# Attention: GpSimd clamps every half tile of the attention in one instruction, VectorE only multiplies, ScalarE only exponentiates

## The reference, cut to what matters

```python
q = (embeds[rows] @ qW).reshape(e, HEADS, dh)        # 4 heads of 24
k = (embeds[cols] @ kW).reshape(e, HEADS, dh)
v = (embeds[cols] @ vW).reshape(e, HEADS, dh)
scores = jnp.clip(jnp.einsum('ehd,ehd->eh', q, k), -10.0, 10.0)
exp_s = jnp.exp(scores)
norms = segment_sum(exp_s, rows)[rows]
w = exp_s / (norms + 1e-08)
res = segment_sum(w[:, :, None] * v, rows)
```

## Time and profile before

| what | us |
|---|---|
| median of 3 runs (lowest, highest) | 1285.33 (1283.32, 1286.96) |
| the profiled execution's own time | 1289.9 |
| its span, first to last instruction | 1287.9 |
| from the attention's first clamp to the end of GpSimd's last one | 450.9 |

### The profile page before, as it was taken

The page is one execution under the profiler, slowest core; times in us unless marked ns, Lnnn a source line. Parts: engine busy times, 40 slices in busy tenths (PEclk is TensorE's granted clock), DMA queues, the critical chain, the costliest instruction groups (busy, mean ns, idle before and its releaser), DMA issues.

```text
span 1287.9 us, 23338 instructions
## 1 busy us (share of the span) xinstructions
PE 1053.3 (82%) x8352; PEld 622.0 (48%) x8352; DVE 966.7 (75%) x1603; ACT 692.6 (54%) x903; POOL 597.2 (46%) x343
## 2 busy tenths in 40 slices
PE   3878877778886788888888888994799699999893
PEld 2545545445553222222222222231569699999783
DVE  8668888896664799999999999994865654542566
ACT  7556555555533899999979898992100000001221
POOL 8442454233103799999989998995000000000000
PEclk9878888977687799999989999997899899999896
DMA  0010000000016211121111222221000100010201
GB/s 10 26 40 5 5 8 6 5 5 18 2 42 189 68 38 46 45 49 47 42 44 36 60 52 51 46 59 48 1 1 32 37 29 21 2 33 8 68 28 38
DMA packets 98907, 44.80 MB, mean 35 GB/s; under 512 B 85196, under 2 KB 96716, under 8 KB 98672
## 3 DMA queue, kind: packets, MB, share of 16 engines
q1 hardware_dynamic: 97104, 41.58, 12.2%
q0 software_dynamic: 1696, 1.74, 0.5%
HBM read 30.73 MB, written 12.56 MB: 34 GB/s over the span
## 4 chain that ended last, share of the span: by engine, by line
PE 52%; DVE 25%; issue 12%; ACT 5%; POOL 4%; another core or an unknown queue 2%; DMA 1%; SPq 0%; DVEq 0%; ACTq 0%; POOLq 0%
DVE Eb L1151 16%; PE PS L1325 16%; PE PS L553 11%; PE PS L557 8%; DVE Eb L1145 3%; PE PS L1765 3%; POOL Eb L985 3%; PE PS L1333 2%; PE PS L1075 2%; PE PS L1065 2%; ACT Eb L1116 2%; PE PS L1316 1%; ACT Eb L1118 1%; PE PS L1772 1%
## 5 line engine op out<-in xcount | busy, mean ns | idle before, releaser
L985 POOL TENSOR_SCALAR Eb<-Eb 128x1024 f32<-128x1024 f32 (+4 forms) x175 | 430.8, 2483 | 42.0 <-ACT Eb L1120 40.8
L1151 DVE SCALAR_TENSOR_TENSOR Eb<-Eb,PS 128x1024 f32<-128x1024 f32 (+4 forms) x350 | 366.8, 1084 | 16.4 <-ACT Eb L1118 10.1
L1120 ACT ACTIVATE Eb<-PS,small 128x1024 f32<-128x1024 f32 (+2 forms) x263 | 251.7, 997 | 27.2 <-PE PS L1065 23.4
L593 ACT ACTIVATE CT<-PS 128x500 f32 x313 | 183.5, 587 | 147.1 <-PE PS L557 139.3
L553 PE MATMUL PS<-mov,oneS 128*128 128x100 f16 x1565 | 187.8, 235 | 74.1 <-issue 70.5
L553 PEld LDWEIGHTS PS<-mov,oneS 128*128 128x128 f16 x1565 | 148.4, 109 | 159.1 <-issue 118.0
L1325 PE MATMUL PS<-hs,CT 128*128 128x192 f16 (+1 forms) x2500 | 213.5, 247 | 3.6 <-DVE SG L1566 1.6
L1325 PEld LDWEIGHTS PS<-hs,CT 128*128 128x128 f16 (+1 forms) x2500 | 208.1, 99 | 7.3 <-DVE SG L1566 2.4
L1065 PE MATMUL PS<-Qb,Kb 96*128 96x512 f16 (+3 forms) x700 | 184.9, 368 | 10.5 <-ACT Eb L1120 6.8
L435 DVE TENSOR_TENSOR oneS<-iotaX,KL 128x2560 f16<-128x2560 int16 x80 | 120.0, 1500 | 75.1 <-PE PS L557 73.0
L1075 PE MATMUL PS<-Eb,V 128*25 128x512 f32 (+3 forms) x1400 | 170.8, 560 | 3.4 <-DVE Eb L1151 1.8
(11 more groups left out here) (278 smaller groups left out, 1017.3 us busy)
## 6 DMA issues: line engine op xcount, KB each, us to landing
Kb<-kd SPq DMA_DIRECT2D x168, 96.0 KB, 2.3
qd<-QH SPq DMA_DIRECT2D x12, 192.0 KB
kd<-QH SPq DMA_DIRECT2D x12, 192.0 KB
hs<-t_d SPq DMA_DIRECT2D x12, 192.0 KB, 2.5
Qb<-qd SPq DMA_DIRECT2D x4, 384.0 KB, 3.8
CT<-x_d SPq DMA_DIRECT2D x1, 1200.0 KB, 9.1
x_d<-B SPq DMA_DIRECT2D x6, 192.0 KB, 1.9
t_d<-A SPq DMA_DIRECT2D x6, 192.0 KB, 1.8
```

Of the source, the lines that this page charges most:

```text
L593: a.activation(K.CT[:, :, bass.ds(words[g % 4][0], GI * W)], K.bank(g % 4)[:, 0:25 * GI * W].rearrange("p (a c) -> p a c", a=25), ACT.Copy ...
L985: g.tensor_scalar(e, e, ELO, None, ALU.max).then_inc(S("floored"), 1)
L1120: a.activation(e, ps, ACT.Exp, scale=K.unsc[0:r, :]).then_inc(S("score_read"), 1)
L1151: v.scalar_tensor_tensor(out=e, in0=e, scalar=EHI, in1=cn, op0=ALU.min, op1=ALU.mult).then_inc(S("weighed"), 1)
```

## The change

GpSimd now takes both halves of every iteration and both bounds, in one `tensor_scalar` with two operations (min with `EHI`, then max with `ELO`). ScalarE runs one plain exponential for each half tile. VectorE's product becomes a `tensor_tensor` without the clamp, in the order half 0, half 1, each waiting for GpSimd's clamp of that half; its own lower clamps, the table `FLOOR`, and the constants `ten` go. TensorE's and SyncE's code is the same but for the name of the semaphore `score_read`, now `score_exp`.

```diff
-FLOOR = [("P", "A") if it % 2 else ("P", "D") for it in range(7 * NT)]
@@ attn_gpsimd
         for k in range(2):
-            if FLOOR[it][k] == "P":
-                e = K.Eb[0:r, (2 * it + k) % NE_, :, 0:wb]
-                g.wait_ge(S("score_read"), 2 * it + k + 1)
-                g.tensor_scalar(e, e, ELO, None, ALU.max).then_inc(S("floored"), 1)
-    g.wait_ge(S("floored"), halves("P", len(ITS)))
+            e = K.Eb[0:r, (2 * it + k) % NE_, :, 0:wb]
+            g.wait_ge(S("score_exp"), 2 * it + k + 1)
+            g.tensor_scalar(e, e, EHI, ELO, ALU.min, ALU.max).then_inc(S("clamped"), 1)
+    g.wait_ge(S("clamped"), 2 * len(ITS))
@@ attn_scalar
-            if FLOOR[it][k] == "A":
-                a.activation(e, ps, ACT.Relu, bias=K.ten[0:r, 0:1], scale=K.unsc[0:r, :]).then_inc(S("score_read"), 1)
-                a.wait_ge(S("score_read"), 2 * it + k + 1)
-                a.activation(e, e, ACT.Exp, bias=K.ten[0:r, 1:2]).then_inc(S("exp_a"), 1)
-            else:
-                a.activation(e, ps, ACT.Exp, scale=K.unsc[0:r, :]).then_inc(S("score_read"), 1)
+            a.activation(e, ps, ACT.Exp, scale=K.unsc[0:r, :]).then_inc(S("score_exp"), 1)
@@ attn_vector, weigh
-        for k in ((1, 0) if FLOOR[it][0] == "P" else (0, 1)):
+        for k in range(2):
             e = K.Eb[0:r, (2 * it + k) % NE_, :, 0:wb]
-            kind = FLOOR[it][k]
-            if kind == "D":
-                v.wait_ge(S("score_read"), 2 * it + k + 1)
-                v.tensor_scalar(e, e, ELO, None, ALU.max).then_inc(step, own.up())
-                v.wait_ge(step, own.n)
-            elif kind == "P":
-                v.wait_ge(S("floored"), halves("P", it))
-            else:
-                v.wait_ge(S("exp_a"), halves("A", it))
-            v.scalar_tensor_tensor(out=e, in0=e, scalar=EHI, in1=cn, op0=ALU.min, op1=ALU.mult).then_inc(S("weighed"), 1)
+            v.wait_ge(S("clamped"), 2 * it + k + 1)
+            v.tensor_tensor(e, e, cn, ALU.mult).then_inc(S("weighed"), 1)
```

More of the change, by code:

```diff
@@ L933 @@
 NK = 3
-FLOOR = [("P", "A") if it % 2 else ("P", "D") for it in range(7 * NT)]
-def halves(kind, it):
-    return sum(f.count(kind) for f in FLOOR[:it + 1])
 B0, BN = (0, 4, 8, 12, 16, 19, 22), (4, 4, 4, 4, 3, 3, 3)
@@ L951, in alloc_attn @@
     K.xb = sb(st, "xb", [128, 1, 4, D], F32)
-    K.ten = K.small[:, 100:102]
     K.rec = K.small[:, 104:136].rearrange("p (k c) -> p k c", k=2)
@@ L1060, in score @@
         if it:
-            p.wait_ge(S("score_read"), 2 * (it - 1) + k + 1)
+            p.wait_ge(S("score_exp"), 2 * (it - 1) + k + 1)
         p.wait_ge(S("k_in%d" % (it % NK)), 16 * (it // NK + 1))
@@ L1114, in attn_scalar @@
                 a.wait_ge(S("valued"), it - 3 + 1)
-            if FLOOR[it][k] == "A":
-                a.activation(e, ps, ACT.Relu, bias=K.ten[0:r, 0:1], scale=K.unsc[0:r, :]).then_inc(S("score_read"), 1)
-                a.wait_ge(S("score_read"), 2 * it + k + 1)
-                a.activation(e, e, ACT.Exp, bias=K.ten[0:r, 1:2]).then_inc(S("exp_a"), 1)
-            else:
-                a.activation(e, ps, ACT.Exp, scale=K.unsc[0:r, :]).then_inc(S("score_read"), 1)
-    a.wait_ge(S("score_read"), 2 * len(ITS))
-    a.wait_ge(S("exp_a"), halves("A", len(ITS)))
+            a.activation(e, ps, ACT.Exp, scale=K.unsc[0:r, :]).then_inc(S("score_exp"), 1)
+    a.wait_ge(S("score_exp"), 2 * len(ITS))
 def attn_vector(v, K):
@@ L1127, in attn_vector @@
     step = own.sem
-    v.memset(K.ten[:, 0:1], 10.0)
-    v.memset(K.ten[:, 1:2], -10.0).then_inc(step, own.up())
     v.memset(K.accS[:, :], 0.0).then_inc(step, own.up())
```

## The result

The change makes the kernel faster: 1210.91 us median (1209.75 to 1212.34, 4 runs) against 1286.14 (1283.32 to 1290.36, 4 runs), a ratio of 0.9408, 95% interval 0.9388 to 0.9427. The forecast was 1692 us, slower; the range from 1615 to 2210 does not hold the time. The rival of the lean two-operation instruction is what happened.

The account below looks back on a forecast made before the run. GpSimd's clamps were to bound the attention: its stretch from 450.9 to 856 us, +405, second operation free, on 1289.9 gives 1695; the runs' median lies 4.6 lower, 1690, said as 1692 us. Range 1615 to 2210.

Parts of the forecast that it names:

- The rival of the lean two-operation instruction: Attention, GpSimd's clamp: two given numbers run as a streaming loop, stage about 400 us, total about 1235 us; chance 14%.
- The bound of the kernel before: Attention: GpSimd, VectorE and ScalarE within 4% of each other, all at 93 to 96% of 450.9 us.
- The price of a one-operation clamp: GpSimd's one-operation tensor_scalar: 215 ns fixed plus 2.49 ns an element, whatever the operation.
- Part 2: GpSimd's clamp in the attention: second operation most likely adds zero; at the upper bound 1.64 ns an element, +514 us.
- Part 1: GpSimd's second half tile in the attention: 350 clamps in place of 175, 856 us busy in place of 430.8.
- part 3: Attention: 856 us of GpSimd clamps in a row set the stage; GpSimd never starves, savings on ScalarE and VectorE worth nothing.
- One sign: Expected new profile of the attention: VectorE, ScalarE and TensorE under 50% busy, all waiting in the end for GpSimd's clamp.
- The small term for VectorE's clamps: Attention: with VectorE's clamps gone, GpSimd's lose their disturbance, 3 us over the present stage; 350 clamps 856 in place of 861.6.
- the 63 us: VectorE's 63.0 us of clamps in the attention, of which the port rule would return up to 63 us; forecast rejected that.
- Its point of decision: GpSimd's two-operation clamp at 1.20 ns an element, 1.44 us a full half tile, keeps the stage at 450.9 us.
- Start, end and the other stages: First clamp starts as before, the end is the same to within 0.3 us, everything before 424 and after the attention unchanged.

Follow-up runs that it names:

- the pair alone: Kernel before with only GpSimd's 175 clamps made two-operation (min, then max), clamps still divided over three engines: 1281.48 us, ratio 0.9960.
- VectorE freed: Kernel before with GpSimd's clamps as min-max and VectorE's clamps given to GpSimd too, ScalarE keeping its own: 1271.97 us, ratio 0.9944.
- ScalarE freed: Kernel before with GpSimd's clamps as min-max and ScalarE's clamps given to GpSimd too, VectorE keeping its own: 1271.46 us, ratio 0.9938.
- the probe: Changed kernel plus 72 unused GpSimd tensor_scalar instructions of 18 forms ahead of the attention, then 15 more forms likewise; only durations count.
- one-operation run: Changed kernel with GpSimd doing only the lower clamp (max) on every half tile, VectorE min and product in one: 1682.79 us, ratio 1.3073.

## Why the prediction was wrong

**The bound of the kernel before: right, and it mattered.** Three engines within 4% of each other was the right reading of the earlier trace rows: the pair alone, with VectorE freed or with ScalarE freed, gave 0.4 to 0.6%; all together 5.9%, and 2.5% where VectorE waits for both clamps.

**The price of a one-operation clamp: right where it was measured.** 215 ns + 2.49 ns an element; the probe gives 206 + 2.50. But "whatever the operation" was said of one-operation forms and then carried on to two.

**Part 2 is the step that failed.** I wrote that the second operation costs "zero for the likeliest, because the line above shows that the loop costs the same whichever operation is in it, as a loop does that always passes through both stages". There is no one price. The probe splits the 186 ns between L212's form and L217's (717 - 531) into 75 for the fetched value and 111 for the second operation. So in the common two-operation form the second one is not free either (3.33 against 2.50 ns an element), and by that price the forecast would have been about 1950; max-min, which has it, measured 1932. The changed kernel's pair is on neither line: 0.83 ns an element, 350 clamps 321.5 us in place of 856. The mistake was to let the rows of other operations, one at a time or as another pair, stand for this pair, with the earlier trace rows showing that GpSimd can run at 0.6 to 0.85 ns an element in other instructions.

**Part 1 and part 3: right as mechanisms for that price.** The one-operation run ended at 1683 against 1692: 350 instructions in a row, GpSimd never starved. Of the 12 us too many, 9 come from adding up durations: the 350 add up to 852.6 us but take 843.8 in a row, since one starts a little before the one ahead has ended. One sign was off even at that price: TensorE was to be under 50% busy, and it was busy 570 of 844 us, at a mean granted clock of 0.68.

**The small term for VectorE's clamps: too small, and read from one row.** The forecast took 5.6 us off for 350 clamps (861.6 to 856). In the one-operation run, with no clamp on VectorE, they take 843.8, so up to 17.8 come off, and a full-width clamp is 2.754 us in place of 2.799. It does not make the clamp dear, but the disturbance is more than the 3 us that I took from the earlier trace rows. There VectorE's clamp starts 1.2 us after one of GpSimd's, as most do, and neither is lengthened by more than 0.02. Others in the same trace are: VectorE's clamp takes up to 1.53 us in place of 0.69 and GpSimd's up to 3.31 in place of 2.76. So my sentence that the trace does not agree with the port rule of the Trainium skill ("SBUF — State Buffer", section "Who interferes with whom") was half right. That the one blocks the other for the whole instruction agrees with the cheap pair's meetings, 1.46 us for 0.69 and 1.38 for 1.04 in the run with the pair alone; with the one-operation clamp it does not hold at every moment, and the 63 us are not in the trace. What the meetings cost the kernel in all, no run isolates.

**The rival of the lean instruction: right in place and condition, and given 14%.** Its point of decision, 1.44 us for a full half tile, was passed with 1.04. Its time, 1235, was 24 too high, since it took TensorE's 390 us as fixed. They are not: TensorE was busy 362.6 us for the same matmuls. About 9 of the 28 us are shorter matmuls (the busy times of TensorE's lines add up to 417 us in place of 426), at a granted clock of 0.99 in place of 0.97; the rest is that with fewer waits the matmuls of one line overlap those of the next more, and overlaps are counted once. VectorE's 366 came first, near the 370 that the rival had for it. What the rival did not see is the pair itself: nothing before the result showed which pairs are lean, so having it in the list was caution more than insight. The rule of the Trainium skill in "GPSIMD Engine Reference", "Engine selection", that one-input elementwise work is roughly line-rate, holds here for min-max, 0.83 ns an element, and does not for one operation, 2.50, or max-min, 3.32. It pointed to the right side of this result, but would have pointed there for the reverse order too, which is 50% slower than before.

**Start, end and the other stages: right.** The time from VectorE's last product to the end of the span is 411.8 us against 410.5, and it varies from 405 to 412 in the traces of the experiments; the start of the attention varies by 8.

## What to carry to other kernels

An instruction that the trace does not show is not priced by its neighbours on GpSimd: the same tensor_scalar costs 0.83, 2.5 or 3.3 ns an element by which operations it has and in which order, so its cost has to be measured, or its range taken from the fastest row of the engine to the slowest. A clamp there is written min first, then max, and a lone scaling could be tried as mult-mult with 1. Where three engines are level, relieving one or two of them gives next to nothing and the gain comes with the last; a cheap step that is not a bound in itself is worth what it lets the others give away. How finely the next engine waits counts as much: here more than half of the gain is lost when VectorE waits for both half tiles at once.

## What the runs showed of the hardware that was not expected

- GpSimd's tensor_scalar on f32, 1024 elements: 1.04 us for min-max, mult-add, add-mult, mult-mult; 2.76 for max, min, mult or add alone; 3.6 for max-min, max-max, min-min, min-add, max-mult, mult-max, mult-min, add-max, add-add, mult-subtract, subtract-mult, subtract-add, is_ge-mult. A second operation can make an instruction 2.7 times faster.
- A value fetched from a tensor in place of a given number costs 76 ns for each instruction there, at 128 as at 1024 elements.
- A clamp of VectorE (0.69 us, SBUF to SBUF) and a min-max clamp of GpSimd (1.04 us) that meet take turns: the one that comes second is lengthened, VectorE's to as much as 1.54 us (run with ScalarE freed), GpSimd's to as much as 1.46 (run with the pair alone). Beside the one-operation clamp most of VectorE's clamps pass unhindered, some wait to its end (up to 1.53 us, in the trace of the kernel before).
- VectorE's product of 2048 elements saves 0.07 us against two of 1024 in an unbroken row; the duration of a single row (2.29 us) does not show it.
